# Earlier token normalization on VectorE, an earlier transpose of the first tokens, and a push taken ahead of a round's last gating

## The reference

```
x = _layernorm(x + _L0_attn_ref(x, ...))   # conv, silu, scan over 8 states, gate, W_out
x = _layernorm(x + _L0_ffn_ref(x, w))      # x @ sign(w).T
x = _layernorm(x + _L1_attn_ref(x, ...))   # 16 heads, s = exp(g) * s + k^T v, o = q s
x = _layernorm(x + _L1_ffn_ref(x, ...))    # top-2 of 8 experts
```

## Time and profile before

| what | value |
|---|---|
| median of three timed runs | 2445.73 us |
| profiled execution, its own time | 2441.41 us |
| its span | 2439.5 us |
| PE, DVE, ACT, POOL busy | 2100.3, 1952.2, 1417.7, 800.3 us |
| granted PE clock, mean | 0.949 of full speed |
| loop round, from one stage-6 gating to the next | 115.12 to 118.39 us |

### The profile page before, as it was taken

How to read it: one execution, slowest core, us unless ns; L and a number is a source line. 1 busy time by engine, 2 the same in 40 slices (tenths; PEclk the granted TensorE clock), 3 DMA queues, 4 the chain that set the end, 5 groups by cost and what they waited for, 6 DMA issues and landing times. The chain is left out here.

```text
span 2439.5 us, 52395 instructions
## 1 busy us (share of the span) xinstructions
PE 2100.3 (86%) x15864; PEld 1548.8 (63%) x15865; DVE 1952.2 (80%) x3681; ACT 1417.7 (58%) x3240; POOL 800.3 (33%) x1060
## 2 busy tenths in 40 slices
PE   4589989898989898989898989889889759999980
PEld 2256656575656575757565656656576659999980
DVE  6687988888888989797989798988885457777768
ACT  3466666676766666666666666666656413333334
POOL 0011415141424233242424141514142234334337
PEclk8699999999999999999999999999999979999995
DMA  6342424334232434242425152424330042222216
GB/s 176 87 114 59 116 73 98 87 82 104 65 104 65 115 79 108 66 112 66 110 59 122 47 125 61 113 71 98 91 76 21 28 154 58 58 59 58 58 56 193
DMA packets 154382, 212.88 MB, mean 87 GB/s; under 512 B 20296, under 2 KB 88912, under 8 KB 153920
## 3 DMA queue, kind: packets, MB, share of 16 engines
q1 hardware_dynamic: 132048, 144.20, 20.1%
q0 software_dynamic: 22272, 67.92, 13.6%
HBM read 134.71 MB, written 28.08 MB: 67 GB/s over the span
## 5 line engine op out<-in xcount | busy, mean ns | idle before, releaser
L1441 DVE TENSOR_TENSOR_SCAN hs<-decay,push 128x512 f32<-128x512 f32 x256 | 312.8, 1244 | 7.1
L1190 ACT ACTIVATE S<-banks,fall_tok 128x128 f32<-128x128 f32 x1024 | 278.8, 385 | 27.7 <-PE banks L823 25.4
L1011 PE MATMUL banks<-rowsT,w_here 128*128 128x128 f32 x2176 | 269.3, 277 | 7.0 <-DVE w_here L1785 6.5
L1011 PEld LDWEIGHTS banks<-rowsT,w_here 128*128 128x128 f32 x2176 | 255.6, 193 | 10.6 <-issue 9.4
L1865 POOL DMA_DIRECT2D y<-ch x96 | 88.3, 920 | 453.3 <-DVE ch L1449 351.0
L1956 POOL TENSOR_TENSOR qd<-q,q_fall 128x512 f32<-128x512 f32 x96 | 158.7, 1653 | 223.6 <-ACT chunk_fall L1175 223.6
L1549 DVE TENSOR_TENSOR S<-banks,S 128x512 f32<-128x512 f32 x256 | 167.5, 684 | 73.4 <-PE banks L835 46.9
L1997 POOL DMA_INDIRECT results_scratch<-rows_out,result_to x136 | 132.2, 972 | 240.8 <-ACT rows_out L1316 233.8
L1305 ACT ACTIVATE tanh_h<-banks 128x512 f32<-128x512 f32 x136 | 81.3, 598 | 203.7 <-PE banks L1011 169.6
L1556 DVE SCALAR_TENSOR_TENSOR oT<-tog,banks 128x512 f32<-128x512 f32 x128 | 87.3, 682 | 135.9 <-ACT sq L1158 135.8
L835 PE MATMUL banks<-q,k 64*128 64x128 f32 x1024 | 149.5, 287 | 44.0 <-DVE state L1600 29.0
(11 more groups left out here) (218 smaller groups left out, 5120.7 us busy)
## 6 DMA issues: line engine op xcount, KB each, us to landing
y<-ch POOLq DMA_DIRECT2D x96, 512.0 KB
b_all<-bc_scratch SPq DMA_DIRECT2D x128, 256.0 KB, 4.9
c_all<-bc_scratch SPq DMA_DIRECT2D x128, 256.0 KB
q_fall<-fall_scratch SPq DMA_DIRECT2D x192, 128.0 KB, 3.2
rows_in<-rows_scratch SPq DMA_DIRECT2D x136, 66.0 KB
both<-results_scratch SPq DMA_DIRECT2D x32, 256.0 KB, 3.4
w<-w_dram SPq DMA_DIRECT2D x3, 2048.0 KB, 8.9
xT<-xT_dram SPq DMA_DIRECT2D x16, 256.0 KB, 2.9
```

Source lines behind the costliest of these rows:

```text
L1011: mm = pe.matmul(bank_h[:, u % 2, n, here], w_here[:, u % 2, n, here], x, start=True, stop=True)
L1190: ins = nc.scalar.activation(S[:, g, here], bank[:, here], ACT.Exp, bias=fall_tok[:, head:head + 1])
L1441: nc.vector.tensor_tensor_scan(hs[:, h, :], decay[:, n % 2, h, :], push[:, h, :], 0.0, ALU.mult, ALU.add).then_inc(s_scan, 1)
```

## The change

Four edits, no operation added or taken away:

1. `normalize` of x1 (stage 5) and of x2_new (stage 7) stand at the start of their stage on DVE, ahead of `gate_out`.
2. PE transposes x1 at the end of its stage 5, ahead of `outputs(5)`, and ACT copies it in its stage 5, behind the masks of the stage. The uses between it and ffn move on by one bank.
3. The push of state 0 of the next sequence is taken out of the round's beginning and stands at the end of the round before, ahead of the last `gate_out`.
4. Nothing changes in the programs of POOL and SP but the banks that POOL waits for.

```
-STATE_OUT = {"mix": 4, "x1T": 6, "ffn": 6}
+STATE_OUT = {"mix": 4, "x1T": 5, "ffn": 6}
...
             def state_scans(n, i):
-                if n == 0:
-                    state_part(0, 0, i)
                 state_part(n, 1, i)
                 state_part(n, 2, i)
...
             def stage(h, i, j, n):
                 m = STATE_IN_STAGE.get(h) if i is not None else None
+                if i is not None and h == NORM_STAGE:
+                    normalize(x1, s_rstd0, s_x1, i)
+                if i is not None and h == NORM2_STAGE:
+                    normalize(x2_new, s_rstd1, s_x2, i)
                 if j is not None:
                     if h:
                         gate_out(h - 1, j)
...
-                    if h == NORM_STAGE:
-                        normalize(x1, s_rstd0, s_x1, i)
...
-                    if h == NORM2_STAGE:
-                        normalize(x2_new, s_rstd1, s_x2, i)
...
                 for h in range(STAGES):
                     stage(h, i, j, n)
+                if n is not None:
+                    state_part(0, 0, n)
                 if j is not None:
                     gate_out(STAGES - 1, j)
```

## The result

The changed kernel takes 2411.19 us (median of four runs, 2408.81 to 2413.9), the kernel before, run beside it, 2445.5 us (four runs, 2438.68 to 2450.8). The ratio is 0.9871, 95% interval 0.985 to 0.9892. The profiled execution took 2408.81 us, its span 2406.9; before it was 2441.41 and 2439.5, so 32.6 us went out of the span. The gain of 1.3% is clear of no change by its interval. The kernel before varies: beside the experiments, 45 undisturbed executions of it took 2438.57 to 2455.53 us (medians of four sessions 2451.55, 2442.25, 2449.02 and 2450.59), the longer ones on the whole at a lower granted clock (0.95 at 2438.57, 0.943 at 2455.53). Its profiled execution is one of the quickest, so a comparison of profiles is likely to understate what is gained in clock.

The account below looks back on a forecast made before the run. Neither PE nor DVE was taken to fill the round; their waits for each other bound it. 0.8 + 1.1 = 1.9 us in 15 rounds (28.5) plus 6.5 of clock made 35, so 2411 us; range 2398 to 2430.

Parts of the forecast that it names:

- The sum: Whole program: 1.9 us a round in 15 rounds, 28.5 us, plus 6.5 us of clock, together 35 us, giving 2411 us.
- x2_new ahead of the gating: Stage 7 on DVE: normalization fits idle time with 0.6 us over; PE's 1.01 us gap at the next round's beginning goes, 1.1.
- x1 turned sooner: Stages 5 to 7: x1 normalized in DVE's idle time, transposed earlier; PE's wait ahead of the sign product goes, 0.8 us.
- the score banks: Stage 6: new need of both score banks falls on DVE's masked scores; priced at nothing, 0.8 us if it bites.
- the 113.2 forecast: Sign to look for: a loop round with clock 1.00 takes 113.2 us; 114 to 115 would make the forecast wrong.
- The push: End of round on DVE: push waits 0.4 us for b_all, then gating; the scan starts 1.55 us sooner.
- the 6.8 at which the rival began to lose: Slower push rival, chance 0.04: from a b_all landing of 6.8 us each microsecond costs one in 14 rounds; 2456 at 7.5.
- it holds, by nothing: Unit 0 on DVE: scan 1.55 us sooner plus 0.34 to spare gives 1.89, against a residual 1.9 us sooner on PE's side.
- DVE under POOL's qd: Stages 5 and 6: x1's normalization takes 1.10 us instead of 2.06; qd then lies over delta and du, so the stretch moves.
- The clock: Round's beginning: with the gap ahead of the copy gone, most falls there go; 6.5 us taken of 17.9.
- the rival that the clock takes its share back: All rounds: the shorter round meets the clock's falls elsewhere; 28.5 - 9.5 = 19 us gained, 2427 us; chance 0.15.

Follow-up runs that it names:

- the first tokens alone: Against the kernel before: x1 normalized ahead of the stage-5 gating and transposed in stage 5, x2_new and the push as before; 2440.55 us, ratio 0.995.

## Why the prediction was right

- **The sum.** 35 us were forecast, 32.6 came in the profiled executions and 34.3 between the medians. The interval of the ratio, 0.985 to 0.9892, makes 2409 to 2419 us of 2445.5, and 2411 lies in it. That it came out to 0.2 us is luck: the order gave 1.65 us in each of 15 rounds, 24.8 and not 28.5, and the rest gave 7.9 and not 6.5; the profiled execution took 2408.81 where 2406.4 was forecast, and the median stood 2.4 us above it instead of 4.3.
- **x2_new ahead of the gating, 1.1 us a round: right.** The gap of 1.01 is gone, and DVE had 0.80 us to spare where 0.6 was worked out. With both normalizations alone a round at full clock is 0.9 us shorter, of which x1's has some 0.2. The loop's branch shows in no row of PE there.
- **x1 turned sooner, 0.8 us a round: the term that was mis-sized.** The gap ahead of the sign product is gone, x1 was ready in its idle time, and the copy delays no squares. But the transpose went into bank 3, which the state update of the same stage (L1596) drains 0.49 us too late. The prediction spoke of the score banks, where nothing came, and passed over this bank, although the row of the new order says that it waits for drained3. 0.8 less 0.49 would leave 0.3, and with the first tokens alone a round is some 0.6 shorter by the estimate above; either way the term is short of 0.8, and the order as a whole gave 1.65 and not 1.9. The round at full clock took 113.49 and not the 113.2 forecast. Turned behind the outputs the wait is gone and a round of one kind is 0.1 to 0.4 shorter (113.12 at full clock), the rest being held back by the push's wait.
- **The push: its timing right, its worth small.** It waited in 5 of 13 rounds, 2.6 us in all, 0.2 a round where 0.4 was taken. The landing of 6.9 us, above the 6.8 at which the rival began to lose, was not one of state 0's row: SP issued it 37.6 us into a round. The residual's wait was 0.35 in rounds without a fall at their beginning before and is 0 to 0.5 now, so "it holds, by nothing" was so (its sum fell from 16.7 to 3.2 us, but seven waits of 2.0 us or more of the 16.7 lay in rounds with a fall at their beginning). The edit itself is worth 0.2 to 0.3 us a round by the traces, and the execution times don't show it. What the push would cost if its row came later is seen where the row is late: nothing up to a wait of some 0.6 us, and about one us for one beyond.
- **DVE under POOL's qd.** x1's normalization now takes 1.12, and du, which lies under a qd of 1.50 us (POOL 1119.44), takes 2.17 or 2.18 in 14 of 16 sequences, where it took 1.22 or 1.23 in all 16 before: the stretch only moved, as taken. The Trainium skill, in "GPSIMD Engine Reference", section 1 (Specifications), says that GpSimd contends with VectorE instructions that have two inputs in SBUF, and the trace agrees.
- **The clock, 6.5 us: near in size, wrong in its reason.** Over 13 rounds of the profiled pair the order gave 13 x 1.65 = 21.5 of the 25.2 us, so the clock gave 3.8; the first and the last round brought 7.4 where the forecast had 2 x 1.9 + 0.9 = 4.7, and how much of that is clock stays open. The prediction said that falls at the round's beginning go because the gap there goes. They went (seven in 13 rounds before, none after), and at +34, where one costs 1.6 as well, there are six instead of two. The first tokens alone show that the falls leave the beginning though its gap stays; two large matmuls in that gap show that closing it is enough to move them; only when the places at +34 are closed too do they end at +52, where a fall costs 0.1 to 0.2. In this pair the rival that the clock takes its share back was more than half true: of 16.3 us (1513.09 - 13 x 115.14) that lay over rounds at full clock before, 12.5 (1487.85 - 13 x 113.49) are still paid. The middle of the 45 executions of before lies some 8 us above its profiled one, at a lower granted clock, so in an average execution the clock probably gave more.

A version that beats both kernels came of it: x1 turned behind outputs(5), 0.9822 of before, and with three large matmuls in the units 2397.39 us, 0.9788.

## What to carry to other kernels

A step that is moved ahead in the order also takes another bank; look up who drained that bank last for every moved use, not only for the tiles it reads. When such a wait is taken away, look at the next one that doesn't move with it, here the transfer of b_all. Where a loop's rounds alternate between two lengths at different clocks, find the gap at which the clock falls before pricing a gap's removal: closing it moved the fall here from +2 to +34, where it costs as much, and only closing the next places too left it where it is cheap. And where executions of one kernel differ by 17 us, don't read a difference of a few us from one profile each; compare medians, or rounds of the same kind. An engine that has to stand idle anyway can be given a few large instructions without use, as long as the loop's program doesn't grow so far that the instruction queue has to bring it again in each round.

## What the runs showed of the hardware

- **A loop's program has a cliff.** With 56 and more PE instructions added to a round of 780 matmuls and 780 weight loads, each loop round stood still for up to 6.5 us at its head, and the instruction queue moved 109 packets more of some 16 KB, about eight for each loop round; with some 24 more it didn't. Filling two idle gaps that way cost 105 us (2547.03 against 2442.25), 63 of them in that wait and part of the rest in a low granted clock behind it. The Trainium skill, in "Runtime: NRT & Kernel Launch", section "Instruction fetch mechanics", states blocks of 16 KiB, which the packets fit. It calls the cost of crossing into the next block mostly hidden, and says that a taken branch to instructions that are no longer held stalls the engine until they are fetched. The trace agrees with the second where the round has grown by 56 instructions or more.
- **The clock falls though no gap of PE is longer than 1.9 us** in the loop rounds of the kernel before and the changed one: behind gaps of 1.01 and 0.75 at the round's beginning, of 1.62, 1.47 and 1.27 in the units, or of 1.88 at +51. Which of them is hit differs between kernels of nearly the same gaps: every second round at +2 (before), about every second at +34 (after), every one at +34 (first tokens alone). The price is set by what comes after: 1.6 us at +2 and +34, 0.1 to 0.2 at +52. There the slower work fills a wait: in the changed kernel PE waits 1.5 us ahead of scores (L835) 61 to 64 us into each of the seven rounds without a fall at +52, and not at all in the six with one.
- **A DVE product under a POOL product is stretched**: du 2.17 us instead of 1.23 under a qd of 1.50.
- **Work that nobody reads made the kernel faster**: three matmuls of 512 columns, in gaps, took 9.1 us out of 13 rounds, and five in the kernel before 27.8 us out of its median.
